# Gate and up in three column ranges, graph counts added behind later tiles, one piece of keys per group

## The reference, cut to what matters

```python
xn = layernorm(x)
# graph layer, twice: h @ W_self + mean of the neighbours @ W_neigh + b, relu between
agg = segment_sum(h[src], dst); mean = agg / max(degree, 1)
# attention: Q, K = elu(xn W + b) + 1, V = Q * sum(K*value) / (Q*sum(K) + 1e-6), gelu(V Wo + bo)
x = x + gnn(xn) + mix(xn)
# feed-forward on layernorm(x), weights of 4 bits in blocks, activations of 16 bits:
xq = qdq(layernorm(x)); up = qdq(xq @ w_up.T); gate = qdq(xq @ w_gate.T)
o = qdq(qdq(gate * qdq_u16(sigmoid(gate))) * up); x = x + o @ w_down.T
```

## Time and profile before

| | us |
|---|---|
| median of three runs | 1212.84 |
| the profiled execution, by its own time | 1213.64 |
| its span in the trace | 1211.8 |
| TensorE (PE) busy | 1157.4 (96%) |
| VectorE (DVE) busy | 679.4 (56%) |
| GpSimd (POOL) busy | 393.2 (32%) |
| ScalarE (ACT) busy | 356.5 (29%) |

### The profile page before, as it was taken

How to read it: one execution, slowest core, us unless ns; L and a number is a source line. 1 busy time by engine, 2 the same in 40 slices (tenths; PEclk the granted TensorE clock), 3 DMA queues, 4 the chain that set the end, 5 groups by cost and what they waited for, 6 DMA issues and landing times.

```text
span 1211.8 us, 15245 instructions
## 1 busy us (share of the span) xinstructions
PE 1157.4 (96%) x6309; PEld 622.7 (51%) x6309; DVE 679.4 (56%) x1232; ACT 356.5 (29%) x446; POOL 393.2 (32%) x224
## 2 busy tenths in 40 slices
PE   4898999999999999995999999999999999999978
PEld 3554555555555554442444555444444445569934
DVE  7766947658475563335633444656564345582763
ACT  5634333333324323310521112222210012251640
POOL 1266767758677684677400000000000000000000
PEclk8999999999999999998999999999999999999989
DMA  9935344353442439532731034432220080000005
GB/s 259 339 81 140 65 100 99 71 135 50 103 85 37 98 71 311 128 53 58 271 109 39 22 116 162 127 105 88 87 87 35 18 156 1 1 1 1 2 8 161
DMA packets 156151, 117.61 MB, mean 97 GB/s; under 512 B 93401, under 2 KB 132569, under 8 KB 155058
## 3 DMA queue, kind: packets, MB, share of 16 engines
q1 hardware_dynamic: 86744, 103.41, 27.4%
q0 software_dynamic: 69024, 13.07, 8.4%
q10 hardware_dynamic: 314, 0.16, 0.0%
HBM read 90.13 MB, written 21.41 MB: 92 GB/s over the span
## 4 chain that ended last, share of the span: by engine, by line
PE 50%; DMA 21%; issue 14%; POOL 12%; DVE 2%; ACT 1%; SPq 0%; POOLq 0%; ACTq 0%; DVEq 0%
PE ps L1053 25%; DMA at_scratch<-copies,cell 18%; POOL at_scratch L598 12%; PE ps L1085 7%; PE ps L1114 6%; PE ps L1151 6%; PE ps L1181 3%; DMA at_scratch<-zeros 2%; DMA raw<-in_L_mix_Wk_dram 1%; PE ps L1123 1%; PE ps L1101 1%; PE ps L991 0%; DMA parts<-at_scratch 0%; POOL at_scratch L588 0%; DMA key_scratch<-key_r 0%
## 5 line engine op out<-in xcount | busy, mean ns | idle before, releaser
L598 POOL DMA_INDIRECT at_scratch<-copies,cell x160 | 345.6, 2160 | 173.6 <-DMA at_scratch<-copies,cell 93.7
L983 PE MATMUL ps<-xnT,whl 128*128 128x512 f16 (+1 forms) x2160 | 383.3, 340 | 0.0
L983 PEld LDWEIGHTS ps<-xnT,whl 128*128 128x128 f16 x2160 | 211.1, 98 | 169.9 <-issue 1.7
L1053 PE MATMUL ps<-hb,hT 128*128 128x512 f16 x960 | 207.7, 379 | 1.3 <-DVE hT L1516 1.3
L1053 PEld LDWEIGHTS ps<-hb,hT 128*128 128x128 f16 x960 | 93.9, 98 | 114.5 <-DVE hT L1516 1.8
L1053 PE MATMUL ps<-hb,xnT 128*128 128x512 f16 x480 | 105.9, 383 | 12.4 <-DVE hb L1386 12.4
L579 POOL PARTITION_ALL_REDUCE ag_fw<-am_fw x9 | 3.2, 354 | 317.0 <-DVE am_fw L1399 317.0
L1053 PE MATMUL ps<-hb,VT 128*128 128x512 f16 x480 | 103.9, 379 | 1.5 <-ACT S_b L740 1.5
L1085 PE MATMUL ps<-AT,P 125*128 125x512 f16 (+1 forms) x480 | 84.7, 339 | 0.0
L1053 PEld LDWEIGHTS ps<-hb,xnT 128*128 128x128 f16 x480 | 47.3, 99 | 69.9 <-DVE hb L1386 12.9
L1114 PE MATMUL ps<-P,AT 125*128 125x512 f16 x360 | 79.0, 379 | 0.0
(11 more groups left out here) (231 smaller groups left out, 1190.1 us busy)
## 6 DMA issues: line engine op xcount, KB each, us to landing
raw<-in_L_gnn_W_neigh_dram SPq DMA_DIRECT2D x32, 512.0 KB, 5.0
raw<-in_L_gnn_W_self_dram SPq DMA_DIRECT2D x24, 512.0 KB, 5.2
key_b<-key_scratch SPq DMA_DIRECT2D x8, 1250.0 KB, 8.8
raw<-in_L_mix_Wo_dram SPq DMA_DIRECT2D x16, 512.0 KB, 3.9
parts<-at_scratch POOLq DMA_DIRECT2D x20, 312.5 KB, 3.8
at_scratch<-zeros POOLq DMA_DIRECT2D x6, 1020.0 KB, 17.7
x_all<-in_x_dram SPq DMA_DIRECT2D x9, 512.0 KB
x_acc<-in_x_dram SPq DMA_DIRECT2D x9, 512.0 KB
```

Of the source, the lines that this page charges most:

```text
L598: pool.indirect_dma_start(out=at_scr[c % 2][:, :], out_offset=bass.IndirectOffsetOnAxis(ap=cell[:, c:c + 1], axis=0), in_=copies[:, c:c + ...
L983: mm = pe.matmul(acc_of(c)[:, a:b], whl[:, i, wp, k, :], xnT[:, k, ap, a:b], start=(k == 0 and wp == 0 and ap == 0), stop=(k == KC - 1 and ...
L1053: mm = pe.matmul(half_bank(i), stationary[:, k, ap, t * TP:t * TP + P], hb[:, n % 2, k, wp, :], start=(k == 0 and wp == 0 and ap == 0), st ...
```

## The change

The column ranges of gate and up become 0 to 375, 375 to 875 and 875 to 1250 instead of five of 250. The pieces in which the codes are made follow: three pieces for the first range (chunks 0-1, 2-4, 5-7), then columns in steps of 250, 250, 250 and 125. In stage one, group g now does one piece of cells (p = g + 1) and does it behind the last `chunk_lo` of the group instead of before it; group 0 did two. The counts are added behind tiles 21 to 34 instead of 15 to 31, the degrees three tiles later. Up's first range is read out behind the second sigmoid, its maxima are taken behind the codes of the gated product.

```diff
-    FCOLS = [(a, a + 2 * TP) for a in range(0, N, 2 * TP)]
+    FCOLS = [(0, 3 * TP), (3 * TP, 7 * TP), (7 * TP, N)]
-    PIECES = [(0, 0, KC // 2), (0, KC // 2, KC)] + [(r, 0, KC) for r in range(1, NR_F)]
-    PIECE_AT = [(1, 2)] + [(g + 2,) if g + 2 < NPC else () for g in range(1, KC)]
+    PIECES = [(0, 3 * TP, 0, 2), (0, 3 * TP, 2, 5), (0, 3 * TP, 5, KC)] + [
+        (a * TP, b * TP, 0, KC) for a, b in ((3, 5), (5, 7), (7, 9), (9, NT))]
+    CODED = [3, 5, 7]
+    FIRST_CODED = [k0 for _, _, k0, _ in PIECES[:CODED[0]]]
+    PIECE_AT = [(g + 1,) if g + 1 < NPC else () for g in range(KC)]
-        DEG_TILE = 33
+        DEG_TILE = 36
-        PART_TILE = {i: s for s, i in enumerate((15, 17, 19, 21, 23, 25, 27, 29, 30, 31))}
+        PART_TILE = {i: s for s, i in enumerate((21, 22, 24, 25, 27, 28, 30, 31, 33, 34))}
...  ScalarE, behind the sigmoid of block c
-                ug_out(NR_F + c)
+                if c == 1:
+                    ug_out(NR_F)
...
-            ug_out(2 * NR_F - 2)
-            ug_out(2 * NR_F - 1)
+            for n in range(NR_F + 1, 2 * NR_F):
+                ug_out(n)
...  TensorE
-                    pe.wait_ge(c_lo, r + 2)
+                    pe.wait_ge(c_lo, CODED[r])
-                        if n == 0 and b == 0 and k % (KC // 2) == 0:
-                            pe.wait_ge(c_lo, k // (KC // 2) + 1)
+                        if n == 0 and b == 0 and k in FIRST_CODED:
+                            pe.wait_ge(c_lo, FIRST_CODED.index(k) + 1)
...  VectorE, group g of stage one
                 v_low(g)
+                if g + 1 < KC:
+                    chunk_lo(g + 1, 3)
                 for p in PIECE_AT[g]:
                     cells(p)
-                if g + 1 < KC:
-                    chunk_lo(g + 1, 3)
-                else:
+                if g + 1 == KC:
...  VectorE, codes
-                dve.wait_ge(xt2_free, 2 * (r + 1))
+                dve.wait_ge(xt2_free, b // TP)
...  VectorE, maxima of up
-                ug_max(NR_F + c)
...
-            ug_max(2 * NR_F - 2)
+            for n in range(NR_F, 2 * NR_F - 1):
+                ug_max(n)
```

More of the change, by code:

```diff
@@ L854, in code_high @@
             def code_high(n):
-                r, k0, k1 = PIECES[n]
-                a, b = FCOLS[r]
+                a, b, k0, k1 = PIECES[n]
                 act.wait_ge(c_lin, n + 1)
```

## The result

The changed kernel takes 1199.76 us in the median of four runs (1198.71 to 1202.06), against 1212.59 before (a fourth run of it, 1212.34, is now counted in); the ratio is 0.9896 (95% interval 0.9879 to 0.9913). The forecast was 1197.1, with 1193.0 to 1203.5. The profiled execution took 1198.71 (span 1196.9), 14.9 less than the one of before; 15.7 was forecast for that.

What follows compares the result with a forecast made beforehand. TensorE, busy 96% of the span, was taken to bound the kernel. -7.4 - 14.0 + 5.6 + 0.1 = -15.7 on the profiled 1213.64 gave 1197.9, and a median of 1197.1 us, range 1193 to 1203.5.

Steps and rivals of the forecast that it cites:

- Stage one, -7.4: Stage one: the earlier low half removes TensorE's 5.78 us wait for squares and 1.6 us of lower clock.
- (d): Rival: scatter starved or crowded, ending later, so TensorE waits at tile 28; 1217 at 50 us late; chance 3%.
- The counts, -14.0: Stage two: counts taken up later remove TensorE's 12.41 us wait for a weight half and 1.6 us of lower clock.
- POOL beside VectorE: Stage two: POOL's b1 additions hold up VectorE's first counts; cost 0, as TensorE has 12 and 4 us of cover.
- The degrees, +5.6: Behind tile 39: TensorE waits 4.6 us for the later reciprocal, plus 1.0 us for the lower clock.
- Gate and up, +0.1: Feed-forward: shorter matmul time, -0.8, offset by code waits, +0.5, and longer read-outs, +0.2; taken as +0.1 us.
- Median: Whole kernel: the median of the runs is 0.8 us below the profiled execution's 1197.9, so 1197.1.

Runs made afterwards that it cites:

- keys_late: order_only, with SP also holding each piece of keys from the third on until the cells of the piece before are done; 1200.39 us, ratio 0.9887.
- pieces_only: The kernel before with one piece of cells in each group, still ahead of the last low half; 1212.65 us, ratio 1.0001.
- warm: The changed kernel with 20 matmuls into an unused PSUM bank ahead of TensorE's wait for the reciprocal; 1196.87 us, ratio 0.9872.
- after: The changed kernel itself, with all edits, against the kernel before; 1199.76 us, ratio 0.9896.
- deg35: The changed kernel with the degrees one tile earlier, at 35, and the last counts moved earlier to match; 1192.16 us, ratio 0.9820.
- counts_only: The kernel before with only the counts behind tiles 21 to 34 and the degrees at 36; 1206.83 us, ratio 0.9937.
- order_only: The kernel before with only the last low half of a group put ahead of the cells, group 0 still doing two pieces; 1206.34 us, ratio 0.9954.

## Why the prediction was right, point by point

**Stage one, -7.4.** Right as a step of TensorE. The low half's load went out at 96.08 (97.4 forecast), the last square ended near 107 (107.0), the wait went. Wrong was the sentence behind it, "I cost the scatter at nothing: it ends at 555 as before, and that is set by POOL and DMA, not by TensorE". It ended 12 us sooner, and no rival had that: (d) only had it later. Part of it comes from SP's key loads, which the same edit moves (keys_late); the rest is open. In the prediction I had noted that SP's wait for the keys moves a group later, and asked only who is queued behind it, not which scatters wait for these loads.

**The counts, -14.0.** Right: with stage one's 7.4 it makes 21.4 against 22.3 measured. Not right was to treat the two as terms of their own. The kernel before hung on the scatter, 659 us from its end; taken alone, stage one's step wins nothing through TensorE (pieces_only), and 13 us through the scatter. Only the later counts cut that tie, and then TensorE's waits add up. Since the changed kernel no longer hangs on the scatter, the sum came out though the scatter was forecast wrongly. That its late end as forecast would have done no harm either is argued, not shown: the reads were to begin 4.5 us behind tile 20's start (554.6 against 550.1), and in all six traces with the later counts they begin 4.7 to 7.1 us ahead of it.

**POOL beside VectorE.** The mechanism is there, the place was not. POOL's six additions ended at 558.5, as the scatter was early, so the first counts took 0.80 us and were not held up. Two weight halves were, with 3.21 and 4.01 us instead of 1.28. The last half ended at 573.2 and the last norm at 592.6, and TensorE wants them at 601.1: 28 and 8.5 us of cover, where I gave 12 and 4, but with a scatter that ended early.

**The degrees, +5.6.** The wait was 4.53 us, forecast 4.6. The clock behind it was mis-sized: 1.0 taken, 2.4 between the traces of warm and after and 2.9 between the medians of warm and after. I scaled it down because the stall was shorter than the other two; the trace has a window of 5 us at 0.50 behind it, where the windows behind the other two have 0.69, so it cost more, not less.

**Gate and up, +0.1.** The start came 0.6 us sooner as forecast (3.7 us behind the maximum instead of 4.3; the row's 0.73 us is the wait ahead of it). The two waits that follow were 0.94 and 0.80, 1.7 together against the forecast 1.9. Up's stream was 38.41 us (38.2), the sum +0.4.

**Median.** The profiled execution was 0.8 above its forecast, the median 2.7: I had taken it 0.8 below the profiled one, as before, and it came out 1.1 above, since the other three runs take 1.0 to 3.4 us longer. The clock behind the reciprocal's wait is the likely cause. Kernels without that loss, deg35 and warm, spread by 0.9 and 1.0 us, counts_only, which has the wait, by 4.2; and the mean granted clock of the other three runs of after is 0.990 or 0.991, against 0.994 in the profiled one. Where it fell in them no trace shows.

## What to carry to other kernels

When another chain (here the scatter) runs beside a busy TensorE for hundreds of us, look for the place where they are tied (here the counts behind tile 15): until it is cut, gains upstream of it on the busy engine are waited for again, as the 5.78 us were in order_only, and once it is cut they count. A step moved later takes its tail along: the reciprocal of 8 us had 11 us of cover at tile 35 and lacked 4.5 at tile 38, and one tile earlier it cost nothing. A moved wait on a DMA queue also moves the transfers behind it: ask which other transfers land later or sooner for it.

## What the runs showed of the hardware that I had not expected

- The time from the first read of the counts to the end was the same to 1 us in seven kernels that add them behind tile 15 (658.9 to 659.9), while their reads began anywhere from 539.9 to 555.9 us. The kernel before ran from 1205.1 to 1219.5 over the four sets; that this spread too is the end of the 160 small scatters is inferred, as only one of its runs has a trace.
- Holding a 1.25 MB load 2.5 to 5.5 us longer, five times, made the kernel 6 us faster in the median, through scatters that ended sooner.
- A wait of TensorE of 4.5 us was followed by 5 us at 1.2 GHz, and filling it with 20 idle matmuls won 2.9 us in the medians and 2.4 in the traces.
